# Halves for the last group's maxima and exponentials, and new instruction orders, in a one-core decoder layer

## What is computed

```python
x = x + _L0_attn_ref(_layernorm(x), conv_w, wq, wkg, wv, wg, bg, wout, aug_balance)
x = x + _L0_xattn_ref(_layernorm(x), ctx_1024, ctx_1024, mask, Wq, Wk, Wv, Wo)
x = x + _L0_ffn_ref(_layernorm(x), w_router, w_block)
# cross-attention, where the halves are made:
scores = jnp.einsum('bhqd,bhkd->bhqk', q, k) / jnp.sqrt(jnp.float32(Dk))
attn = jax.nn.softmax(scores, axis=-1)
ctx = jnp.einsum('bhqk,bhkd->bhqd', attn, v)
```

## Time and profile before

| | |
|---|---|
| median of 3 runs | 339.26 us (339.2 to 339.34) |
| the profiled execution's own time | 339.64 us |
| its span, first to last instruction | 337.9 us |
| mean granted TensorE clock | 0.966 of full |
| PE / DVE / ACT / POOL busy | 290.5 / 253.6 / 245.5 / 171.1 us |
| x_scores(n,0) of n = 1 to 7 start at | 78.40, 113.3, 147.98, 182.57, 217.3, 251.71, 283.47 us |

### The profile page before, as it was taken

One profiled execution on the slowest core, in us unless ns is written; L12 is line 12 of the kernel. 1 busy time (PEld: TensorE's weight loads), 2 busy tenths in 40 slices (PEclk: granted clock), 3 DMA queues, 4 the chain that ended last, 5 costly groups with the idle time before them and its releaser, 6 DMA issues.

```text
span 337.9 us, 9707 instructions
## 1 busy us (share of the span) xinstructions
PE 290.5 (86%) x3672; PEld 209.1 (62%) x3672; DVE 253.6 (75%) x604; ACT 245.5 (73%) x438; POOL 171.1 (51%) x226
## 2 busy tenths in 40 slices
PE   5648777999798989998999899999998998888872
PEld 4536636766577657855786568656865675466551
DVE  2697799569857978798879887987778665647544
ACT  4596967786976798679867986888688866682611
POOL 5154275753457448743875287617661454024420
PEclk9898799999999999999999999999999999999975
DMA  3820300020003000210020001200210001001010
GB/s 75 238 68 2 95 2 2 12 71 2 0 14 78 9 3 8 66 41 2 10 65 10 2 6 53 57 0 7 57 34 2 8 11 44 2 2 31 2 31 16
DMA packets 15726, 10.46 MB, mean 31 GB/s; under 512 B 2816, under 2 KB 13952, under 8 KB 15680
## 3 DMA queue, kind: packets, MB, share of 16 engines
q1 hardware_dynamic: 15680, 9.84, 10.9%
HBM read 4.79 MB, written 2.10 MB: 20 GB/s over the span
## 4 chain that ended last, share of the span: by engine, by line
PE 40%; ACT 19%; issue 17%; DVE 11%; POOL 7%; SPq 4%; DMA 1%; POOLq 0%; ACTq 0%; DVEq 0%
PE S L816 6%; PE PT L853 6%; PE PB L874 6%; PE AT L739 4%; ACT k_bd L1137 4%; PE PA L758 3%; SPq L278 3%; PE S L831 3%; ACT pr L1249 3%; ACT L1173 2%; PE PB L795 2%; PE PA L639 2%; DVE q_bd L1549 2%; DVE nmax L1617 2%; PE PA L774 2%
## 5 line engine op out<-in xcount | busy, mean ns | idle before, releaser
L1617 DVE TENSOR_REDUCE nmax<-S 128x16 bf16<-128x1024 f32 x31 | 37.9, 1223 | 16.0 <-PE S L816 15.7
L1256 ACT COPY prT<-PT 128x512 f32<-128x512 f32 x62 | 36.2, 584 | 16.7 <-PE PT L853 10.7
L1249 ACT ACTIVATE pr<-S,rs 128x1024 f32<-128x1024 f32 x31 | 34.7, 1119 | 15.7 <-PE S L831 15.3
L853 PE MATMUL PT<-ident,pr 128*128 128x128 f32 x248 | 39.1, 280 | 4.1 <-ACT prT L1256 2.2
L1137 ACT ACTIVATE k_bd<-S,k_rows 128x512 f32<-128x512 f32 (+1 forms) x72 | 40.8, 655 | 2.0 <-DVE k_rows L1728 1.6
L816 PE MATMUL S<-k_bd,qT 64*64 64x512 f32 x248 | 33.8, 615 | 8.0 <-ACT pr L1249 7.6
L874 PEld LDWEIGHTS PB<-v_x,prT 128*64 128x64 f32 x992 | 33.7, 137 | 10.0 <-issue 8.8
L874 PE MATMUL PB<-v_x,prT 128*64 128x18 f32 x992 | 39.0, 213 | 0.9 <-DVE cx L1630 0.7
L853 PEld LDWEIGHTS PT<-ident,pr 128*128 128x128 f32 x248 | 26.9, 140 | 20.0 <-issue 9.5
L486 POOL TENSOR_TENSOR kc<-ke,e_r 128x512 f32<-128x512 f32 x32 | 34.2, 1082 | 6.0 <-issue 5.7
L739 PE MATMUL AT<-q_bd,kc 128*64 128x128 f32 x512 | 32.0, 278 | 2.7 <-DVE z L1569 1.8
(11 more groups left out here) (170 smaller groups left out, 702.2 us busy)
## 6 DMA issues: line engine op xcount, KB each, us to landing
cT<-in_ctxT SPq DMA_DIRECT2D x7, 256.0 KB, 3.1
v_bd<-vt SPq DMA_DIRECT2D x28, 64.0 KB, 2.1
out<-yout SPq DMA_DIRECT2D x7, 256.0 KB, 2.2
q_bd<-qs SPq DMA_DIRECT2D x96, 8.0 KB
cT<-in_ctxT SPq DMA_DIRECT2D x2, 128.0 KB, 2.4
x_all<-in_x SPq DMA_DIRECT2D x1, 256.0 KB, 2.9
v_bd<-vt SPq DMA_DIRECT2D x8, 32.0 KB, 2.2
out<-yout SPq DMA_DIRECT2D x2, 128.0 KB, 2.4
```

The costliest lines, as they stand in the source:

```text
L853: last = nc.tensor.transpose(dst[:, P * p:P * p + P], pr_v[:, i % 2, P * (hp * n + p):P * (hp * n + p) + P], ident[:, :])
L1249: nc.scalar.activation(pr_v[:, i % 2, :], s_buf(g, i)[:, :], ACT.Exp, scale=rs2[:, col:col + 1]).then_inc(s_exp, 1)
L1256: nc.scalar.copy(prT[:, 512 * n:512 * n + 512], pt_buf(g, n)[:, :]).then_inc(s_prT, 1)
L1617: nc.vector.tensor_reduce(nmax[:, XH * (i % 2):XH * (i % 2) + XH], cut(s_buf(g, i), XH, L), AX.X, ALU.max, negate=True).then_inc(s_max, 1)
```

## The change

Two things are done. First, in group 8 alone, `b_max` takes the maxima in two instructions of eight heads and 512 columns, `less_half` subtracts one half after its maximum, `b_exp` takes the exponential in two halves, and `x_attend(8,i,n)` waits for its half. `x_scores` of group 8 runs over the column half outside and over the sequence inside, and signals after each column half; the semaphores s_S, s_max, s_fold and s_exp count halves there. Second, the orders of all five engines are written anew: the same functions, called at other places, with step boundaries of PE and POOL drawn elsewhere, so that some calls of `step(n)` now stand at the end of the one before. The diff, cut to its core and to 12 columns less of indent (orders of the opening, of SP and of the closing are left out but for what is told here: on PE the matmuls keep_awake(0,0), (0,2), (0,4) no longer stand ahead of transpose_x(0); on ACT clear_scores(0) has gone from behind a_gates(0) to the front, a_silu(1) stands behind a_er(0), and in `closing` and `last` PE's transpose_o(8) stands ahead of x_scores(7,3) and gla_out(8) ahead of x_attend(7,3,0); on SP each values_to_blocks(g) stands ahead of the store that it followed; in DVE's opening a_stats(4) and a_conv(3,2) are added, from `step(1)`):

```diff
@@ -527,101 +527,108 @@
...
 def step(n):
-    a = n + 2
-    keys(a, 3)
-    scale_b3(n)
-    center_b3(n)
-    norm_b3(n)
+    a, b = n + 2, n + 1
     if has(a + 1):
-        floors(a + 1)
-    route(n)
-    if has(a + 1):
-        spans(a + 1)
+        scaled_keys(a + 1)
         clipped_spans(a + 1)
-    if has(a + 2):
-        center_a(a + 2)
-    group_norm(a)
-    if has(a + 2):
-        scale_a(a + 2)
-    route2(n)
-    count(n)
+        products(a + 1)
     if has(a + 2):
         norm_a(a + 2)
     if has(a + 1):
-        scaled_keys(a + 1)
-        products(a + 1)
         keys(a + 1, 0)
-        keys(a + 1, 1)
     result(n)
     if has(a + 1):
+        keys(a + 1, 1)
         keys(a + 1, 2)
+        keys(a + 1, 3)
+    center_b3(b)
+    if has(n + 5):
+        scale_a(n + 5)
+    scale_b3(b)
+    norm_b3(b)
     scale_b2(a)
+    route(b)
+    if has(n + 5):
+        center_a(n + 5)
+    if has(a + 2):
+        floors(a + 2)
+    if has(a + 1):
+        group_norm(a + 1)
+    route2(b)
+    if has(a + 2):
+        spans(a + 2)
+    count(b)
...
@@ -809,13 +816,22 @@
     else:
         pe.wait_ge(s_exp, start(g) + i - 1)
     dst = s_buf(g, i)
+    def run(half, r):
+        b = 2 * i + half
+        rows = slice(RUN * r, RUN * r + RUN)
+        return nc.tensor.matmul(dst[L * half:L * half + L, XHG * L * r:XHG * L * r + XHG * L],
+                                qT[rows, L * b:L * b + L], k_bdv[rows, g % 2, :, L * b:L * b + L],
+                                start=True, stop=False, skip_group_check=True)
+    if g == NG - 1:
+        for r in range(RUNS):
+            run(0, r)
+            run(1, r).then_inc(s_S, 1)
+        return
     for half in range(2):
         for r in range(RUNS):
-            b = 2 * i + half
-            rows = slice(RUN * r, RUN * r + RUN)
-            last = nc.tensor.matmul(dst[L * half:L * half + L, XHG * L * r:XHG * L * r + XHG * L],
-                                    qT[rows, L * b:L * b + L], k_bdv[rows, g % 2, :, L * b:L * b + L],
-                                    start=True, stop=False, skip_group_check=True)
+            last = run(half, r)
     last.then_inc(s_S, 1)
 def less_max(g, i):
@@ -833,12 +849,23 @@
                                 start=False, stop=True, skip_group_check=True)
     last.then_inc(s_fold, 1)
+def less_half(g, i, n):
+    pe.wait_ge(s_max, start(g) + 2 * i + n + 1)
+    hh = XH // 2
+    at_i = XH * (i % 2) + hh * n
+    nc.tensor.matmul(s_buf(g, i)[:, 512 * n:512 * n + 512], ident_b[:, :],
+                     nmax[:, at_i:at_i + hh].unsqueeze(2).to_broadcast([P, hh, L]),
+                     start=False, stop=True, skip_group_check=True).then_inc(s_fold, 1)
 def x_attend(g, i, n):
     if i >= tiles(g):
         return
     hp = PAIRS // 2
-    if n == 0:
+    if g == NG - 1:
+        pe.wait_ge(s_exp, start(g) + 2 * i + n + 1)
+    elif n == 0:
         pe.wait_ge(s_exp, start(g) + i + 1)
     if g < NG - 1 or (i == 0 and n == 0):
         pe.wait_ge(s_prT, 2 * (start(g) + i) + n)
...
 def step(n):
     a, b, c = n + 2, n + 1, n - 1
-    attend(b, 0, 1)
-    attend(b, 1, 0)
-    attend(b, 1, 1)
-    less_max(n, 0)
     project_qk(a)
-    transpose_x2(c)
+    router(c)
     x_scores(n, 1)
-    router(c)
+    x_attend(n, 0, 0)
+    less_max(n, 1)
     project_v(a)
-    less_max(n, 1)
+    x_attend(n, 0, 1)
     project_g(a)
     ffn(c)
-    x_attend(n, 0, 0)
     x_scores(n, 2)
-    x_attend(n, 0, 1)
+    x_attend(n, 1, 0)
     x_values(n, 0, 0)
-    x_attend(n, 1, 0)
+    x_values(n, 0, 1)
     less_max(n, 2)
     transpose_o(b)
     x_attend(n, 1, 1)
-    x_values(n, 0, 1)
+    x_values(n, 1, 0)
     x_scores(n, 3)
     x_attend(n, 2, 0)
-    x_values(n, 1, 0)
     x_values(n, 1, 1)
+    x_attend(n, 2, 1)
     less_max(n, 3)
-    x_attend(n, 2, 1)
-    gla_out(b)
-    x_values(n, 2, 0)
-    x_attend(n, 3, 0)
-    x_values(n, 2, 1)
     if has(a + 1):
         transpose_x(a + 1)
+    x_values(n, 2, 0)
+    x_values(n, 2, 1)
+    x_attend(n, 3, 0)
+    context_keys(a)
     x_attend(n, 3, 1)
     x_values(n, 3, 0)
     aug_weights(a)
     x_values(n, 3, 1)
     context_values(a)
     x_out(n)
-    context_keys(a)
+    gla_out(b)
+    x_out2(n)
     queries(b)
-    x_out2(n)
     scores(a, 0)
     queries2(b)
+    attend(a, 0, 0)
     scores(a, 1)
-    attend(a, 0, 0)
     x_scores(b, 0)
+    attend(a, 0, 1)
+    attend(a, 1, 0)
+    attend(a, 1, 1)
+    transpose_x2(n)
+    less_max(b, 0)
...
+def last():
+    gla_out(8)
     x_attend(7, 3, 0)
     x_values(7, 2, 1)
     x_attend(7, 3, 1)
     x_values(7, 3, 0)
     x_values(7, 3, 1)
-    gla_out(8)
+    keep_awake(8, 20)
     x_out(7)
     x_out2(7)
-    keep_awake(8, 22)
-def last():
     queries(8)
+    keep_awake(8, 21)
     queries2(8)
-    keep_awake(8, 20)
     x_scores(8, 0)
-    keep_awake(8, 21)
     x_scores(8, 1)
-    less_max(8, 0)
+    less_half(8, 0, 0)
+    less_half(8, 0, 1)
     transpose_x2(7)
+    less_half(8, 1, 0)
+    less_half(8, 1, 1)
     router(7)
     ffn(7)
+    keep_awake(8, 23)
+    keep_awake(8, 22)
     x_attend(8, 0, 0)
-    less_max(8, 1)
-    keep_awake(8, 23)
     x_attend(8, 0, 1)
     x_values(8, 0, 0)
+    x_values(8, 0, 1)
     x_attend(8, 1, 0)
     x_attend(8, 1, 1)
-    x_values(8, 0, 1)
     x_values(8, 1, 0)
     x_values(8, 1, 1)
     x_out(8)
+    keep_awake(8, 25)
+    x_out2(8)
     keep_awake(8, 24)
-    x_out2(8)
-    keep_awake(8, 25)
     keep_awake(8, 26)
     transpose_x2(8)
+    router(8)
     ffn(8)
-    router(8)
...
@@ -1242,10 +1273,14 @@
         return
     if i == 0:
         act.wait_ge(s_rs2, g + 1)
+    col = TPG * (g % 2) + i
+    if g == NG - 1:
+        for n in range(2):
+            act.wait_ge(s_fold, start(g) + 2 * i + n + 1)
+            nc.scalar.activation(pr_v[:, i % 2, 512 * n:512 * n + 512], s_buf(g, i)[:, 512 * n:512 * n + 512],
+                                 ACT.Exp, scale=rs2[:, col:col + 1]).then_inc(s_exp, 1)
+        return
     act.wait_ge(s_fold, start(g) + i + 1)
-    col = TPG * (g % 2) + i
-    if g == NG - 1 and i > 1:
-        act.wait_ge(s_PT, 2 * (start(g) + i - 1))
     nc.scalar.activation(pr_v[:, i % 2, :], s_buf(g, i)[:, :], ACT.Exp, scale=rs2[:, col:col + 1]).then_inc(s_exp, 1)
 def b_probs(g, i, n):
...
 def step(n):
     a, b, c = n + 2, n + 1, n - 1
     a_keys(b, 1)
+    a_gate(b)
     b_queries(n)
+    a_keys(b, 2)
+    b_queries2(n)
     a_aug(b)
-    a_keys(b, 2)
     a_keys(b, 3)
-    b_queries2(n)
-    a_gate(b)
     a_silu(a)
+    b_ffn(c)
     b_exp(n, 0)
     a_qk(a)
-    b_ffn(c)
     a_abs(a)
     a_square(b)
     a_ln(a)
+    b_probs(n, 0, 0)
     a_spread(b)
     b_exp(n, 1)
     a_deviation(b)
-    b_probs(n, 0, 0)
-    b_gelu(c)
     b_probs(n, 0, 1)
     a_decay(a)
+    b_gelu(c)
     a_eq(a)
     b_probs(n, 1, 0)
+    a_key(a)
+    a_ek(a)
     b_exp(n, 2)
     b_probs(n, 1, 1)
-    a_ek(a)
-    a_key(a)
-    b_gelu2(c)
+    a_gates(a)
+    a_er(a)
     b_probs(n, 2, 0)
     a_v(a)
+    b_probs(n, 2, 1)
     b_exp(n, 3)
-    b_probs(n, 2, 1)
-    a_er(a)
-    a_gates(a)
+    if has(a + 1):
+        a_features(a + 1)
+    b_gelu2(c)
     b_probs(n, 3, 0)
     b_probs(n, 3, 1)
-    if has(a + 1):
-        a_features(a + 1)
+    a_keys(a, 0)
     b_out(n)
     a_values(a)
-    a_keys(a, 0)
...
@@ -1612,6 +1647,14 @@
 def b_max(g, i):
     if i >= tiles(g):
         return
+    if g == NG - 1:
+        hh = XH // 2
+        for n in range(2):
+            dve.wait_ge(s_S, start(g) + 2 * i + n + 1)
+            at_i = XH * (i % 2) + hh * n
+            nc.vector.tensor_reduce(nmax[:, at_i:at_i + hh], cut(s_buf(g, i)[:, 512 * n:512 * n + 512], hh, L),
+                                    AX.X, ALU.max, negate=True).then_inc(s_max, 1)
+        return
     dve.wait_ge(s_S, start(g) + i + 1)
     dve.wait_ge(s_fold, max(0, start(g) + i - 1))
     nc.vector.tensor_reduce(nmax[:, XH * (i % 2):XH * (i % 2) + XH], cut(s_buf(g, i), XH, L), AX.X, ALU.max, negate=True).then_inc(s_max, 1)
...
@@ -1748,17 +1791,17 @@
 dve.wait_ge(borne, 1)
 def first():
+    taps(0)
     a_stats(0)
     first_norm(0)
-    taps(0)
+    key_rows(0)
     a_conv(0, 0)
     a_conv(0, 1)
+    constants(0)
     a_conv(0, 2)
     a_conv(0, 3)
-    constants(0)
-    ones(0, 0)
+    constants2(0)
     a_stats(1)
-    key_rows(0)
     a_silu(0)
...
 def step(n):
     a, b, c = n + 2, n + 1, n - 1
-    a_conv(a, 2)
     a_conv(a, 3)
     a_mask(b, 1)
     b_max(n, 0)
@@ -1836,75 +1880,77 @@
     a_outputs(b)
     a_sums(b)
     a_center(b)
+    a_gate(b)
+    b_route(c)
     b_max(n, 1)
+    b_own(c)
     a_squares(b)
-    b_route(c)
     a_log(a)
-    a_gate(b)
+    b_ranks(c)
     a_scan(a)
-    if has(a + 1):
-        a_stats(a + 1)
-    b_own(c)
     a_spans(a)
     b_max(n, 2)
-    b_gelu(c)
     a_scaled_q(a)
+    b_weigh(n, 0)
     a_gated(b)
-    b_ranks(c)
-    b_weigh(n, 0)
     b_max(n, 3)
     b_weigh(n, 1)
+    b_gelu(c)
+    if has(a + 2):
+        a_stats(a + 2)
+    b_taken(c)
+    b_weigh(n, 2)
```

(18 more changed lines are left out.)

287 lines of the change are left out of this document (148 added, 139 removed).

## The result

The changed kernel takes 336.1 us (median of 11 runs, 334.31 to 338.92), the kernel before 339.34 beside it; the ratio is 0.9898, 95% interval 0.9873 to 0.9923. The forecast was 341.3, its range 336.3 to 344.5. So it is 1.0% faster, where the forecast's likeliest case was slower. The profiled execution took 334.87, with a span of 333.1, and is one of the fastest: the traces differ by 4.8 us, the medians by 3.2.

The account below looks back on a forecast made before the run. PE was taken to bound the repeated step (32.88 of 34.66 us busy). 339.64 + 1.8 (opening) + 1.4 (steps) - 0.25 (closing) - 0.3 - 0.6 (last group) = 341.7, less 0.38: 341.3 us; range 336.3 to 344.5.

Parts of the forecast that it names:

- Part 1: Opening, up to x_scores(1,0): about 1.8 us slower, bounds +0.5 to +2.6.
- the stall: Opening: DVE's constants2(0), moved ahead of a_stats(1), stands 1.65 us for w_later; a_silu(0) comes 1.75 late.
- Part 2: The repeated step: about 0.25 us slower each, 5.7 times, +1.4; period 34.9.
- the rule weighed in the forecast: Step: a two-SBUF-input DVE instruction contends with SBUF-reading GpSimd; by it the tap takes 1.1, the step 0.35 longer than taken.
- Part 3: Closing: about 0.25 us faster; x_scores(7,0) 0.4 earlier, x_out(7) 0.25 earlier.
- Part 4: Last group: about 0.3 us faster up to x_out(8), 0.6 faster behind it.
- (a): Step: both new PE waits, 0.8 and 0.9, are halved; period 34.0, total 336.1; chance 0.25.
- (b): Opening swallows its stall, step even, end stays: -1.15, 338.1, up to 339.9 with half the stall; chance 0.18.
- (c): Step: POOL becomes the bound, 0.65 us more in each at the upper lengths, total 345.0; chance 0.10.
- (d): Opening: without the early matmuls more runs at a lowered PE clock, about 2 us more, 343.3; chance 0.07.

Follow-up runs that it names:

- e13: Kernel before with DVE's constants2(0) moved directly behind constants(0), so that it waits for w_later there; 341.59 us, ratio 1.0048.
- e3: Changed kernel with DVE's constants2(0) moved back behind a_stats(2), so that DVE no longer stands for w_later; 333.3 us, ratio 0.9815.
- e4: Kernel before with ACT's a_qk(2) moved behind b_exp(0,0) and POOL's keys(1,0) ahead of floors(2); 338.43 us, ratio 0.9958.
- e9: Kernel of e3 with POOL's keys(1,1) to keys(1,3) moved ahead of floors(2); 334.25 us, ratio 0.9846.
- e7: Kernel of e3 with DVE's key_rows(0) behind a_stats(1) again and ACT's a_keys(0,1) ahead of a_qk(0); 333.94 us.
- e2: Changed kernel with the last group's scores, maxima, subtractions and exponentials whole again instead of in halves; 335.19 us, ratio 0.9864.
- e5: Kernel of e3 with PE's project_v(a) moved ahead of less_max(n,1) in the step; 333.83 us.
- e12: Kernel of e3 with ACT's a_keys(a,0) behind b_out(n) and a_values(a) in the step, as in the kernel before; 336.23 us, ratio 0.9911.
- e11: Kernel of e3 with PE's router(8) behind ffn(8) in the last group, as in the kernel before; 334.19 us.
- e10: Changed kernel with keep_awake(0,0), (0,2) and (0,4) ahead of transpose_x(0) on PE again; 335.7 us, ratio 0.9895.
- e8: Kernel of e3 with ACT's a_qk(2) ahead of b_exp(0,0) again; 335.52 us.
- e15: Changed kernel with three more keep_awake calls (twelve matmuls) ahead of project_qk(0) on PE; 334.94 us, ratio 0.9842.
- e1: Kernel before with the changed orders of first and opening on every queue, all else as before; 338.79 us, ratio 0.9978.

## Why the forecast was wrong

The measured 336.1 us lies just below the range.

**Part 1** had its one priced term right: the stall was put at 1.75 at a_silu(0) and 1.8 at x_scores(1,0), e13 measured 2.02 and 1.98, e3 2.2 by the trace. What failed is the sentence that first_blocks(1,1), "4.78 us, ends at about 53.4": a length of the old trace was carried over, though the rows of POOL beside it showed why it was long, and the diff moved POOL. The kc was the cause, worth 1.5 to 1.6 us (e4, e9). The second miss is a_keys: the forecast gave its move 0.35, as the copy of qk(0) comes sooner; with key_rows(0) and all that follows it was 1.4 (e7). Together they are 3.0 of the 4.2 us that the opening wins without its stall (e3). The other 1.2 lie between scores(0,0) and x_scores(0,0), 17.38 us before and 16.06 in e3; 0.5 of it is scores(0,0) itself, 2.47 us at a granted 0.77 before and 1.97 at 1.00 in e3. What makes the rest stays open; the clock can have a part in it, as it moved x_scores(0,0) by 2.4 between the changed kernel and e2. The clock of the opening, to which the forecast gave only a rival that slows it, is a term that its sum put at nothing.

**Part 2** named the waits rightly and sized two stretches wrongly. The first is from x_scores(n,3) to x_out, put at -0.4 for the x_values that has gone ahead of it, and -0.62 in the mean. The second is from x_out to the next x_scores, put at +0.24 with a wait of 0.8 for the mask, and +0.04 with one of 0.54 in the mean: DVE's lengths were added up in full, but its instructions start some 0.08 before the one ahead has ended, so that the mask starts 4.99 us after x_out in the fourth step and not 5.3. Of PE's waits, that ahead of less_max(n,1) is not on the path at all (e5), since ACT alone sets the time from exp(n,0) to exp(n,1). That for the mask was put at 0.8 in each step and is 0.34 to 0.98; the tap ahead of it, weighed at 0.75 or 1.1, took 1.36 in the second step, beside POOL's kc:
```profile
139.52 1.36 DVE L1534 SCALAR_TENSOR_TENSOR y<-xpad,conv_half,y 128x512 f32<-128x512 f32 x1
```
In the fourth step it is 0.74, alone, and the wait 0.36; in the fifth 0.47, with a smaller group, and the wait 0.34. So the wait is about 0.35 and what POOL adds to the tap. The third step's tap takes 1.05; the rule weighed in the forecast was the right one for the second and third step, and took 0.3 to 0.6 us there. The lengths behind it were misread: the two taps that took 2.19 together were one of 0.73 and one of 1.42, and not 1.1 each. And the wait that goes, 0.57 in the earlier trace rows, is the wrong price of the move: in the new order it would be 1.03, and without the move the steps would be 0.6 longer each (e12). Other instructions are stretched less in the steps too: in the third, yv, gl and the copy under `taken` on DVE are each 0.3 to 0.4 us shorter than before. No run shows whether that is on the path.

**Part 3** came near in its sum, not in its parts. X_scores(7,0) comes 0.46 earlier for 0.4. X_out(7), put at 0.25 earlier, comes 0.03 earlier, as it takes 22.93 us from x_scores(7,0) instead of 22.50; x_scores(8,0) follows it 0.33 sooner.

**Part 4.** Up to x_out(8) it was wrong: put at -0.3, measured +0.18. Exp(8,0) came 4.86 after x_scores(8,0) instead of 4.48, not earlier; the exponential halves are 0.64, as forecast near 0.59; whole again, x_out(8) is where it was before (e2). Behind x_out(8), put at -0.6, the trace has -1.24, but -0.66 against e3 at a like clock (13.47 for 14.13 us), and the router's order is worth 0.7 by itself (e11). So the 0.6 was right in size, with the router's order and not the halves as its cause, and another 0.6 goes with the clock.

**Rivals.** The time of (a), 336.1, is that of the result, but by luck: it had periods of 34.0 and the opening at +1.8. Its waits did shrink, from 0.8 and 0.9 to 0.54 and 0.54 in the mean, but one of them is not on the path; the periods were 34.38 in the mean, and the opening paid most. (b), that the opening swallows its stall, is refuted by e3 and e13; its upper end of 339.9 is that of the whole stall paid, with half it is 339.0. (c) didn't come: exp(n,0) starts 3.73 us after x_scores(n,0) in four of the five full steps, for a forecast 3.8. (d) had the right place, the clock of the opening, and e10 shows no part of the early matmuls in it; the mean clock from 13 to 52 us is 0.87 before and in the changed kernel.

## What to carry to other kernels

A duration taken from the old trace holds only as long as its neighbours stay: before carrying a long instruction over, ask what makes it long, and whether the diff moves that. A wait counts only if no other engine is full over the same stretch, and the wait that a move removes is to be priced in the new order, not in the old. When a change bundles a stall with gains, take the stall out: here 2.8 us lay behind one line. And before two ends are compared, put their granted clocks side by side: of the 1.1 us that the last group seemed to win, 0.6 were the clock.

## What the runs showed of the hardware

The collision of DVE's tensor_scalar and POOL's tensor_tensor is, in these traces, not a slowing by a share but a lock, one instruction at a time. In the kernel before, the first five instructions of first_blocks(1,1), ahead of kc, take 1.53 us:
```profile
46.89 1.53 DVE L1549 TENSOR_SCALAR q_bd<-qs,block_of 128x256 f32<-128x256 f32 x5
```
The other three take the 3.3 us of the three kc, 1.16 at most each: one DVE instruction for each POOL instruction of 1.1. With one kc beside them the eight take 2.83 (e4): one of about 0.9 and seven that follow at 0.27. So an estimate of the price is the time of POOL's instructions less 0.27 for each: 3.26 - 0.8 = 2.5 of the 2.6 measured before, and 1.08 - 0.27 = 0.8 for 0.65 in e4. Kc itself goes from 3.15 to 3.26 at most in that place and 3.63 in e9. The Trainium skill (SBUF — State Buffer, Who interferes with whom) says that a tensor_scalar in a two-port mode and GpSimd exclude each other for a whole instruction, "fully blocks (not throttle)"; the rows agree with that, but none of them names the mode in which q_bd was written.

The clock of the opening differs between executions of one program: the granted clock fell on 16 to 24 us in one and on 28 to 40 in another, and moved x_scores(0,0) by 2.4 us. The 32 matmuls of scores(0,0) take 1.97 us at a granted 1.00, 2.47 at 0.77 (kernel before), and 3.55 to 3.63 at 0.53 and 0.54 (e2, e8, e15). In the steps the clock is full, and the first four come back to 0.05 us. In the last group the same instructions took 27.13 us in the kernel before and 26.27 in e1, where the clock stayed full for some 5 us longer.
